# Stacking the inputs of the 32-token blocks of a state-space stage on 128 partitions, by on-chip transfers

## The reference, cut to what matters

```python
proj = layernorm(x) @ W_in                  # z | x_raw (32 heads x 2 ranks x 8) | B | C | dt | lam | theta
xg = (lam * dt) * silu(x_raw);  xb = ((1 - lam) * dt * alpha) * previous token of silu(x_raw)
sg = einsum('bclgn,bcmgrn->bclmgr', C, B) * SCALE
y_intra = sum over m <= l, r of sg[l, m, r] * dmat[l, m, head] * xg[m, head, r, :]   # and the same with xb
st      = sum over l of dec_end * B * xg ...           # state handed to the next chunk
y_inter = SCALE * C . dec_in * state of the chunks before
y = rms((y_intra + y_inter) * silu(z)) @ W_out
```

## Time and profile before

| what | value |
|---|---|
| median of 3 executions | 1459.83 us (1456.45 to 1460.56) |
| the profiled execution's own time | 1460.59 us |
| its span in the trace | 1458.7 us |
| busy in the span: TensorE, VectorE, ScalarE, GpSimd | 80%, 77%, 55%, 45% |
| mean granted TensorE clock | 0.85 |

### The profile page before, as it was taken

The page is one execution under the profiler, slowest core; times in us unless marked ns, Lnnn a source line. Parts: engine busy times, 40 slices in busy tenths (PEclk is TensorE's granted clock), DMA queues, the critical chain, the costliest instruction groups (busy, mean ns, idle before and its releaser), DMA issues. The chain is left out here.

```text
span 1458.7 us, 33100 instructions
## 1 busy us (share of the span) xinstructions
PE 1172.2 (80%) x11444; PEld 747.4 (51%) x11444; DVE 1118.2 (77%) x2557; ACT 804.6 (55%) x1477; POOL 659.2 (45%) x859
## 2 busy tenths in 40 slices
PE   7679954798898988998739994558987998899894
PEld 7369953455454545554618993444443543443333
DVE  6959963878888888899687995567778878876644
ACT  3768845455145235311347883127876777677881
POOL 2366633753773674365347663353233431521100
PEclk6789985698888898898658997568998999998996
DMA  9035340000000000000502342000000000000000
GB/s 283 11 99 171 89 59 15 26 5 5 20 9 1 23 9 2 2 2 2 197 4 77 90 89 44 15 15 14 2 23 6 19 23 1 16 8 8 1 16 8
DMA packets 55715, 55.11 MB, mean 38 GB/s; under 512 B 9882, under 2 KB 44484, under 8 KB 55556
## 3 DMA queue, kind: packets, MB, share of 16 engines
q1 hardware_dynamic: 46468, 34.37, 7.6%
q0 software_dynamic: 9088, 18.63, 5.7%
HBM read 32.26 MB, written 20.71 MB: 36 GB/s over the span
## 5 line engine op out<-in xcount | busy, mean ns | idle before, releaser
L2137 ACT ACTIVATE l_probs<-l_ps 128x1024 f32<-128x1024 f32 (+1 forms) x320 | 288.0, 946 | 106.6 <-PE l_ps L2023 104.7
L781 POOL DMA_INDIRECT ffn_yg<-y_rows,ffn_index x156 | 156.8, 1005 | 81.5 <-PE ffn_ps_t L796 37.8
L2042 PE MATMUL l_ps<-l_probs,l_vs 128*32 128x512 f32 (+3 forms) x1536 | 167.2, 525 | 28.0 <-DVE l_oTs L2370 16.2
L864 ACT ACTIVATE ffn_hT<-ffn_ps_h,experts_b1T,experts_scales 128x256 f32<-128x256 f32 x312 | 150.8, 562 | 30.5 <-PE ffn_ps_h L811 29.0
L263 POOL DMA_INDIRECT combine_og<-o_rows,combine_place x128 | 139.9, 1093 | 53.8 <-issue 31.4
L1307 PE MATMUL ssm_ps<-ssm_X,ssm_near 32*32 32x256 f32 x2048 | 136.8, 418 | 1.6 <-DVE ssm_Y L1750 1.6
L2361 DVE TENSOR_TENSOR l_probs<-l_probs,last_tri 128x256 f32<-128x256 f32 x256 | 102.5, 438 | 43.0 <-ACT l_probs L2137 41.2
L2023 PE MATMUL l_ps<-l_qkT 32*128 32x512 f16 (+3 forms) x768 | 110.6, 342 | 17.5 <-ACT l_probs L2137 15.4
L889 DVE SCALAR_TENSOR_TENSOR ffn_h<-ffn_hT,experts_scales,ffn_h 128x512 f16<-128x512 f32 x156 | 117.2, 751 | 5.5
L827 PE MATMUL ffn_ps_o<-experts_w,ffn_h 128*128 x624 | 112.8, 220 | 2.1 <-DVE ffn_h L889 1.9
L1549 POOL TENSOR_TENSOR ssm_u_out<-ssm_ysum,ssm_zx 128x256 f32<-128x256 f32 x32 | 69.0, 2157 | 97.7 <-DVE ssm_ysum L1761 97.6
(11 more groups left out here) (352 smaller groups left out, 2977.2 us busy)
## 6 DMA issues: line engine op xcount, KB each, us to landing
o_rows<-ffn_out_sb SPq DMA_DIRECT2D x78, 128.0 KB
y_rows<-ffn_y SPq DMA_DIRECT2D x8, 512.0 KB, 4.9
kept_w<-experts_w SPq DMA_DIRECT2D x16, 256.0 KB
experts_w<-kept_w SPq DMA_DIRECT2D x16, 256.0 KB, 5.9
ffn_yg<-y_rows,ffn_index POOLq DMA_INDIRECT x156
x_res<-in_L_attn_x SPq DMA_DIRECT2D x4, 512.0 KB, 6.1
prep_raw<-in_L_ffn_W SPq DMA_DIRECT2D x1, 2048.0 KB, 10.5
prep_raw<-in_L_ffn_W SPq DMA_DIRECT2D x8, 256.0 KB, 5.8
```

Source lines behind the costliest of these rows:

```text
L781: g_.indirect_dma_start(yg[:, i % RING, j].rearrange("p n d -> p (n d)"), None, w.y_rows.ap(), bass.IndirectOffsetOnAxis(ap=index[:, n:n + ...
L864: s.activation(hT[:, i % 2, c, :], ps_h[:, i % 2, c, :], ACT.Gelu, bias=w.b1T[:, bass.ds(e * HC + c, 1)], scale=SC[:, 6:7]).then_inc(h_rea ...
L2042: ins = t_.matmul(ps_o[VP * h:VP * h + VP, q0 % H:q0 % H + width], vs[:, s % 2, kb, h, :], probs[:, n % PSLOTS, i, at:at + width], start=( ...
L2137: s_.activation(probs[:, w % PSLOTS, i:i + n, 0:width], ps_s[w % 2][:, i:i + n, 0:width], ACT.Exp, scale=SCALE / (UNIT * UNIT)).then_inc(S ...
```

## The change

The two kinds of leaf and the levels 8 and 16 are no longer 32-row products. The inputs that belong to one block of 32 tokens, of two masks (i) and two ranks (r), are put under one another on 128 partitions, in a tile `stacked`, and one product over 128 rows does what four did; for levels 8 and 16 one over 64 rows does what two did.

- `dots` writes the products of a block twice, to partitions r*32 and (2+r)*32 of `ps_near`: 16 products of 64x32x32 in a tile in place of 8.
- `near_levels` masks these in one instruction of the same 256 elements.
- `weigh` on VectorE is three instructions (two of 1024 elements, one of 512) in place of one of 2560, on GpSimd two of 512 in place of one of 1024. The rows that get stacked lie in `X`, which now has one buffer; the others lie in `Xf`, with two.
- SP issues 16 transfers for a tile, each of 32 partitions x 2 x 256 elements (64 KB) from `X` to `stacked`, 8 after each of the first two instructions of `weigh`. `levels` waits for all 16, and so does `weigh` of the next tile.
- `near_level` is 4 products for a call and 3 calls for a tile (12 products, 24 records) in place of 32 (64 records).
- `ysum` lies in `Y6`, so the third `scale` of a tile now waits for GpSimd's `sum_up` of the tile before.
- `SsmWeights.load` fetches W_in in four transfers in place of one, two of which put the ranks apart (pieces of 8 values).

```diff
-    LOADS = 16 * 10
+    LOADS = 16 * 13
@@ load
+        ranks = a["L0_attn_W_in"][:, DI:DI + XR].rearrange("p (h r d) -> p r h d", h=self.H, r=R)
+        for dst, src in ((self.win[:, 0:DI], a["L0_attn_W_in"][:, 0:DI]), (self.win[:, DI + XR:], a["L0_attn_W_in"][:, DI + XR:]),
+                         *((self.win[:, DI * (r + 1):DI * (r + 2)].rearrange("p (h d) -> p h d", h=self.H), ranks[:, r]) for r in range(R)),
...
-        X = sb("X", [P, 2, K_X, XR])
-        near = sb("near", [P, 2, 4, R, BLOCK])
+        X = sb("X", [P, K_N, XR])
+        Xf = sb("Xf", [P, 2, K_X - K_N, XR])
+        stacked = sb("stacked", [P, 2, 2, P // BLOCK, DI])
+        near = sb("near", [P, 2, 2, P // BLOCK, BLOCK])
...
@@ dots
-                        for m in range(0, P, BLOCK):
-                            t_.matmul(o[m:m + 32, 0:32], k[:, m:m + 32], q[:, m:m + 32], start=True, stop=True, skip_group_check=True)
+                        for m in range(P // BLOCK):
+                            block = slice(m * BLOCK, (m + 1) * BLOCK)
+                            for to in (r * BLOCK, (R + r) * BLOCK):
+                                t_.matmul(ps_near[to:to + BLOCK, m, :], k[:, block], q[:, block], start=True, stop=True, skip_group_check=True)
@@ levels
+                def near_level(n, o, kind, rows):
+                    for m in range(P // BLOCK):
+                        ins = t_.matmul(o[m * BLOCK:(m + 1) * BLOCK], near[rows, n % 2, kind, m, :], stacked[rows, n % 2, kind, m, :],
+                                        start=True, stop=True, skip_group_check=True)
+                    return ins
...
+                    pe.wait_ge(S["stacked"], STACKS * (n + 1))
...
-                    for k in range(2):
-                        for r in range(R):
-                            near_level(n, ps_o[0][:, 0:DI], k, k, r, k == 0 and r == 0, k == 1 and r == 1)
-                    for r in range(R):
-                        ins = near_level(n, ps_o[0][:, DI:], 2, 2, r, r == 0, r == 1)
-                    ins.then_inc(S["o_done"], 1)
+                    near_level(n, ps_o[0][:, 0:DI], 0, slice(0, P))
+                    near_level(n, ps_o[0][:, DI:], 1, slice(0, 64)).then_inc(S["o_done"], 1)
...
+                    near_level(n, ps_o[1][:, 0:DI], 1, slice(64, P))
                     for r in range(R):
-                        near_level(n, ps_o[1][:, 0:DI], 3, 3, r, r == 0, r == 1)
@@ weigh on GpSimd
-                    g_.tensor_tensor(X[:, n % 2, K_V:] ... one instruction
+                    for k in range(K_V, K_X):
+                        far_weight(g_, n, k).then_inc(S["x2_ready"], 1)
@@ weigh on VectorE
+                    if n:
+                        dve.wait_ge(S["stacked"], STACKS * n)
+                    q = n % SLOTS
+                    shape = [P, K_N, H, PD]
+                    for r in range(R):
+                        v.tensor_tensor(X[:, :, r * DI:(r + 1) * DI].rearrange("p k (h d) -> p k h d", h=H),
+                                        zx[:, q, (r + 1) * DI:(r + 2) * DI].rearrange("p (h d) -> p h d", h=H).unsqueeze(1).broadcast_to(shape),
+                                        xw[:, q, 0:K_N].unsqueeze(3).broadcast_to(shape), ALU.mult).then_inc(S["x_ready"], 1)
+                    for k in range(K_N, K_V):
+                        far_weight(v, n, k).then_inc(S["x_ready"], 1)
@@ scale
+                            if i == 2:
+                                dve.wait_ge(S["u_ready"], n)
...
+            @block.sync
+            def _(sp):
+                for n in range(TILES):
+                    if n >= 2:
+                        sp.wait_ge(S["o_done"], 3 * (n - 1))
+                    for r in range(R):
+                        sp.wait_ge(S["x_ready"], 3 * n + r + 1)
+                        for i in range(2):
+                            to = (i * R + r) * BLOCK
+                            for m in range(P // BLOCK):
+                                sp.dma_start(stacked[to:to + BLOCK, n % 2, :, m, :],
+                                             X[m * BLOCK:(m + 1) * BLOCK, i:4:2, r * DI:(r + 1) * DI]).then_inc(S["stacked"], 16)
```

More of the change, by code:

```diff
@@ L1301, in weighed @@
                 def weighed(n, k, r, rows):
[L1302 to L1308 removed]
+                    return Xf[rows, n % 2, k - K_N, r * DI:(r + 1) * DI]
+                def near_level(n, o, kind, rows):
+                    for m in range(P // BLOCK):
+                        ins = t_.matmul(o[m * BLOCK:(m + 1) * BLOCK], near[rows, n % 2, kind, m, :], stacked[rows, n % 2, kind, m, :],
+                                        start=True, stop=True, skip_group_check=True)
                     return ins
```

69 lines of the change are left out of this document (32 added, 37 removed).

## The result

| what | before | after |
|---|---|---|
| median of 4 executions each, same chip | 1459.76 us | 1505.69 us (1500.22 to 1510.29) |
| ratio after / before | | 1.0309, 95% interval 1.0280 to 1.0338 |
| span of the profiled execution | 1458.7 us | 1504.5 us |
| mean granted TensorE clock | 0.85 | 0.804 |

The change makes the kernel 3.1% slower: 46 us, where -3.5 were forecast, and it lies outside the range of 1442 to 1480 us.

A forecast was written before the change was run, and what follows sets the result against it. VectorE and TensorE both nearly full in the middle, VectorE the bound in the last tiles. Against 1460.6 us: -22 + 2 + 2 + 4.5 + 5 + 1 + 2 + 2 = -3.5, so 1457 us; range 1442 to 1480.

The forecast's parts named there:

- SP's transfers: Sixteen issues per tile, mostly hidden: +2 us jitter in the last seven tiles, +2 us for second and last tile.
- Rival B: Transfers set the pace, `weigh` waits for the 16 of the tile before: 1471 us, or 1487; chance 0.25.
- TensorE: Shorter level products reach the signals some 1.4 us earlier per tile: -22 us of VectorE's waits; `dots` waits +2 us.
- C: Rival: TensorE's products of 128 rows by 32 columns run singly, the -22 go: 1507 us; chance 0.04.
- -22 + 2 + 2: VectorE's waits for level products -22 us, its waits for `dots` +2, TensorE's lower clock +2.
- Taking turns: VectorE and GpSimd alternate, so `weigh` in three lets GpSimd in twice: +5 us in the middle, +1 in the last tiles.
- +10.5 us: `weigh` in parts: +4.5 us for two more VectorE instructions per tile, +5 and +1 for alternating with GpSimd.
- rival A: VectorE keeps its turn through all of `weigh`, and SP's issues are 0.4 us apart: 1444 us; chance 0.25.
- The clock: TensorE stands idle more and runs at its lower clock more: +2 us, between 0 and 15.
- The load: Three more W_in transfers at the start, 12 us of issue for two, covered by 40 us before `y_rows` is needed: 0.
- the masks: VectorE's masks, like `near` and the sum into `Y6`, keep their elements: nothing.
- the third `scale`: Its new wait for `sum_up` of the tile before is met some 5 us earlier: nothing.

The follow-up runs named there:

- the run through DRAM: Changed kernel, but `X` regrouped by two 512 KB writes to DRAM and eight 128 KB reads per tile: 1523.79 us, ratio 1.0068 to the kernel before.

## Why the prediction was wrong

**SP's transfers: the step that failed.** The sum had a pace of 10.3 us, "1.2 us for its first instruction, 0.1 for the semaphore, 15 spacings of 0.48 = 7.2, and the landing of the last", and +2 and +2 us for it. Measured were 1.3 + 9.6 + 2.2 = 13.0 to 13.3 us. Of the 2.9 missing, 2.4 are the spacing (0.64) and some 0.4 the landing. By the run without transfers the two terms are 3.35% or 49 us, where the sum had 4. The path was right: `weigh` waits for the sixteen of the tile before. Rival B named the mechanism, the point from which it decides (10.3 us), the place (the last tiles) and a price of 7 us for each us beyond: (13.3 - 10.3) x 7 = 21 us, against 21.9. It had a chance of 0.25.

The forecast itself set the pace (10.3) equal to VectorE's own tile (10.3) and then took this margin of nothing as met. The bounds (0.36 to 0.48) came from transfers that start or end in DRAM; that a row is nearest doesn't make it near, and no transfer within SBUF was in the trace. B put its trouble into the landing, up to 4.9 us, and never moved the spacing; the landing was near the short end and the spacing outside. B's far end of 1487 us (its terms add up to 1486, or 1489 with the 3 us for the clock) still fell 19 short, by three terms: the middle (15.8 us of waits where 7 were set), the second `weigh` (6.6 us where it shared 2 with the last tile), and the last tile (5.3).

The middle was judged by the distances of before: five of 23 lie under 13.3 us and would pay 6.5. Nine paid, because the pace itself is longer there: from `weigh` to the end of the wait are 13.6 to 17.2 us in these nine. The longest (VectorE's and SP's timeline, 416 to 435 us):

```profile
416.84 4.67 DVE L1733 TENSOR_TENSOR ssm_X<-ssm_zx,ssm_xw 128x1024 f32<-128x1024 f32 x2 [3.19 <-DMA ssm_stacked<-ssm_X]
420.45 10.41 SPq L1819 DMA_DIRECT2D ssm_stacked<-ssm_X  x16
434.06 1.23 DVE L1733 TENSOR_TENSOR ssm_X<-ssm_zx,ssm_xw 128x1024 f32<-128x1024 f32 x1 [2.76 <-DMA ssm_stacked<-ssm_X]
```

Here the first instruction of `weigh` took 3.5 us in place of 1.2, while GpSimd had its turns, so that the issues began 3.6 us after `weigh`; they took 0.2 us more than in the tile at 647.33; and the last landed 3.8 us after it was issued in place of 2.15. In the other eight it is one or two of these, single issues of up to 1.75 us among them. The pace had no term for any of the three; why issues and landings are longer there is open.

The landing alone would have been right by the figure that the prediction quotes from the Trainium skill, page "DMA: Bandwidth & Descriptors", section "Anatomy of one DMA": 2.0 us + 64 KB / 436 GB/s = 2.15, and the trace has 2.15. The section gives this figure for transfers that GpSimd issues, which the prediction doesn't say; these are SP's, and that it fits them is shown by the trace alone.

**TensorE: right in kind, over twice too large.** The rounds run side by side with 128 rows, and C fell (24 records in 2.12 us at the lower clock). But "the nine tiles that waited longer get 9 x 1.4 = 12.6 us back, the others all" counted the waits of both signals. The products got shorter ahead of the first one alone. The prediction had the two numbers apart (15.5 and 18.6) and added them. The first went to 1.9 and 1.6 us, the second stayed at 18.5 and 17.5: -8 in place of -22 + 2 + 2 (-5 on the faster chip). Why the second wait doesn't shrink when all that stands ahead of it starts earlier wasn't taken apart.

**Taking turns: right for the instruction, wrong for the time.** All signs came in the changed kernel: 14 of the 32 second pieces are longer, 1.75 to 2.1 us and three 3.8, `sum_up` (L1565) takes 1.09 us on average (before 2.16), and the state's decay (L1753) 0.41 in the last tiles. The +10.5 us were measured as +0.9. The middle's share was laid on a path that wasn't VectorE's alone: the busy time grew there by 10.1 us, and its waits for the level products fell by 10.2. The prediction let them swallow 6. (Its rival A has two sizes for what L1731 gives back, 11 us and "some 6", and its terms make 1443 and not 1444; A fell either way, since the turns are taken.)

**The clock.** The clock fell further than thought, to 0.78 in the middle and 0.52 at the end. That isn't the cause of the loss: with eight transfers it was still 0.66 at the end, and the loss was gone. What it costs was measured in no run by itself. The 3 us between the ends of the runs with eight transfers (64.1 us at 0.66) and with none (60.9 at 0.81) are the nearest there is; the transfers are in them too. The +2 can't be told wrong by it.

**The load, the masks, the third `scale`:** nothing that the runs tell from zero; no run has them apart. The 12 us for the issues of the load rest on a row read wrongly. The four of `y_rows` that take 6.03 us start at 28.66, 29.13, 29.61 and 34.37: the last waits for its input, and none is 1.5 us long. In the changed kernel `y_rows` begins 6.4 us later, and the cover of 40 us holds either way.

The sum in hindsight: -8 (products) +1 (parts) +49 (transfers) = +42 us, against 46 measured; with -5 for the products it is 45. The 49 are themselves 46 less the -4 of the run without transfers, so all that the sum tests is whether the parts make that -4.

## What to carry to other kernels

Count issues, not bytes. Where transfers stand in a row on one queue, and a single buffer waits for the last of them, the pace is the number of issues times the issue time plus one landing, here with the DMA engines busy for a third of their time; take the issue time from a transfer of the same kind, and if the trace has none, let the forecast rest on the far bound when the margin is nil. And a shorter piece of work returned only the waits for the signal that closes it, not those for the next one: don't add the two up before the second is followed to its own source.

## What was not expected of the hardware

- From one issue within SBUF to the next SP takes 0.63 to 0.65 us for 32, 64 and 128 KB alike, between DRAM and SBUF 0.47 (the reads in the run through DRAM) and 0.36 to 0.48, with single ones longer (the fourth for `W_in` in the changed kernel takes 3.3). What makes the difference isn't shown. DMA engines were busy for a third of the time only.
- ScalarE's queue has nearly the same price (0.65 us apart), and ScalarE has no other instruction in these 5.2 us.
- In the last tiles TensorE at 0.66 of full speed in place of 0.81 cost at most about 3 us of 61: the ends of the runs with eight transfers and with none differ by that, and by the transfers.
- Of the 24 records of one tile in the changed kernel (from 660.59 us) those of 64 rows started eight at once, within 0.05 us, where those of 128 rows started four at once.
